# Signalling from TensorE by a drain behind each group of matmuls

## The reference

```python
x = layer_norm(dense_t @ Wd.T, gd, bd)                      # 2048 x 128
y = layer_norm(einsum('bnd,ed->bne', sparse_t, Ws), gs, bs)  # 26 rows of 64 -> 26 x 128
y = einsum('bne,pn->bep', y, Wsi)                           # 26 -> 32
y = swapaxes(layer_norm(y, gsi, bsi), 1, 2)
T = concatenate([x[:, None, :], y], axis=1)                 # 33 vectors of 128
Z = einsum('bnd,bmd->bnm', T, T)                            # their products
z = layer_norm(Z[:, TRIL_I, TRIL_J] @ Wl.T, gl, bl)[:, :384]
h = maximum(concatenate([z, dense_t]) @ W_top1 + b_top1, 0)
h = maximum(h @ W_top2 + b_top2, 0)
y = h @ W_top3                                              # 2048 x 1
```

## Time and profile before

| what | value |
|---|---|
| time, median of 3 runs | 772.6 us (771.04 to 772.69) |
| profiled execution, span | 1160.8 us |
| its own time beside the span | none is given |
| TensorE matmuls busy | 677.3 us (58%), 3847 |
| TensorE weight loads busy | 530.5 us (46%), 3847 |
| VectorE busy | 581.9 us (50%) |
| ScalarE busy | 480.7 us (41%) |
| GpSimd busy | 400.3 us (34%) |

### The profile page before, as it was taken

The page is one execution under the profiler, slowest core; times in us unless marked ns, Lnnn a source line. Parts: engine busy times, 40 slices in busy tenths (PEclk is TensorE's granted clock), DMA queues, the critical chain, the costliest instruction groups (busy, mean ns, idle before and its releaser), DMA issues.

```text
span 1160.8 us, 12848 instructions
## 1 busy us (share of the span) xinstructions
PE 677.3 (58%) x3847; PEld 530.5 (46%) x3847; DVE 581.9 (50%) x1124; ACT 480.7 (41%) x1459; POOL 400.3 (34%) x436
## 2 busy tenths in 40 slices
PE   5035446739184672927638374672927558388887
PEld 4023333727164371725517263461715437176664
DVE  4126536627274462727437165452717547188850
ACT  1004634525245252515436154342515526157753
POOL 6735252351705325070431706234070432500000
PEclk9558777969688797878859788795978869689998
DMA  8101010010100001010000101000010000100000
GB/s 312 25 16 18 12 19 11 10 20 3 26 3 17 13 10 21 0 26 3 15 14 3 26 0 21 8 12 17 1 26 2 16 14 8 22 1 1 1 1 1
DMA packets 15585, 22.55 MB, mean 19 GB/s; under 512 B 7461, under 2 KB 8127, under 8 KB 15039
## 3 DMA queue, kind: packets, MB, share of 16 engines
q0 software_dynamic: 13312, 13.66, 6.1%
q1 hardware_dynamic: 2240, 8.50, 2.0%
HBM read 22.12 MB, written 0.01 MB: 19 GB/s over the span
## 4 chain that ended last, share of the span: by engine, by line
PE 33%; another core or an unknown queue 28%; ACT 20%; issue 15%; DVE 4%; ACTq 0%; DVEq 0%
ACT zd L898 14%; PE bank_z L697 10%; PE bank_z L685 7%; ACT mixed L922 4%; PE bank_b L656 3%; PE bank_z L759 2%; PE bank_d L748 2%; PE bank_z L646 2%; PE bank_c L656 2%; PE bank_b L732 1%; PE bank_c L732 1%; DVE y L414 1%; PE bank_c L733 1%; DVE mixed L402 1%
## 5 line engine op out<-in xcount | busy, mean ns | idle before, releaser
L574 POOL DMA_INDIRECT rows<-in_table,ids x416 | 396.3, 953 | 135.0 <-issue 122.7
L898 ACT COPY zd<-bank_z 32x96 f32<-32x96 f32 (+3 forms) x768 | 194.1, 253 | 260.2 <-remote 151.8
L392 DVE COPY zd<-bank_z 32x96 f32<-32x96 f32 (+3 forms) x384 | 103.0, 268 | 212.6 <-remote 151.3
L646 PE MATMUL bank_z<-ident,rows 128*128 128x128 f32 x208 | 44.3, 343 | 278.7 <-ACT zd L898 165.3
L646 PEld LDWEIGHTS bank_z<-ident,rows 128*128 128x128 f32 x208 | 33.5, 181 | 300.5 <-issue 139.9
L568 POOL TENSOR_TENSOR ids<-ids_all,row_base 128x26 int32<-128x26 int32 x16 | 3.8, 236 | 473.9 <-DVE scaled L472 470.9
L697 PE MATMUL bank_z<-wl,zd 128*128 128x512 f32 x288 | 155.9, 675 | 6.6 <-ACT zd L898 6.6
L685 PE MATMUL bank_z<-r_vec 128*128 128x133 f32 x1024 | 135.4, 290 | 27.6 <-ACT zd L898 12.4
L685 PEld LDWEIGHTS bank_z<-r_vec 128*128 128x128 f32 x1024 | 131.2, 202 | 32.5 <-issue 17.0
L906 ACT ACTIVATE y_sq<-y 128x512 f32<-128x512 f32 x128 | 75.3, 625 | 90.0 <-DVE y L414 89.9
L732 PE MATMUL bank_b<-mixed,proj_hi 128*128 128x512 f32 x64 | 46.6, 729 | 100.7 <-DVE y L414 62.2
(11 more groups left out here) (114 smaller groups left out, 1004.0 us busy)
## 6 DMA issues: line engine op xcount, KB each, us to landing
rows<-in_table,ids POOLq DMA_INDIRECT x416
wl<-in_wl SPq DMA_DIRECT2D x1, 2304.0 KB
dense_t<-in_dense_t SPq DMA_DIRECT2D x1, 2048.0 KB
w<-in_w SPq DMA_DIRECT2D x1, 1280.0 KB
wsi_b<-in_wsi_b SPq DMA_DIRECT2D x1, 1248.0 KB
w<-in_w SPq DMA_DIRECT2D x1, 512.0 KB
mask_b<-in_mask_b SPq DMA_DIRECT2D x1, 288.0 KB
ids_all<-in_ids SPq DMA_DIRECT2D x1, 208.0 KB, 2.3
```

The costliest lines, as they stand in the source:

```text
L392: ins = v.tensor_copy(to, src)
L574: nc.gpsimd.indirect_dma_start(rows[par][:, c, D * blk:D * (blk + 1)], None, io["table"], bass.IndirectOffsetOnAxis(ap=ids[par][:, n:n + 1 ...
L646: mm = pe.transpose(bank_t[g % 2][:, n * P:(n + 1) * P], rows[par][:, c, :], ident[:])
L898: ins = nc.scalar.copy(to, src)
```

## The change

In ten helpers of TensorE's `tile_work` the increment is taken off the last matmul (or transposition) and put on a drain instruction that follows it. All are of the same form; these two stand for all ten (`turn`, `gram_product`, `interact`, `linear`, `turn_z`, `mix`, `project`, `first_layer`, `second_layer`, `third_layer`). In `project` there is one drain for each of the two halves; in `linear` and `first_layer` one behind the last piece alone. The waits, the order, the buffers and the matmuls of the set-up are as before.

```diff
                     for n, c in enumerate(GROUPS[g]):
-                        mm = pe.transpose(bank_t[g % 2][:, n * P:(n + 1) * P], rows[par][:, c, :], ident[:])
-                    mm.then_inc(turned, 1)
+                        pe.transpose(bank_t[g % 2][:, n * P:(n + 1) * P], rows[par][:, c, :], ident[:])
+                    pe.drain().then_inc(turned, 1)
...
                         pe.matmul(bank_g[blk][:], proj_hi[:], mixed[:, j % 2, blk, :], start=True, stop=False)
-                        pe.matmul(bank_g[blk][:], proj_lo[:], mixed[:, j % 2, blk, :], start=False, stop=True)\
-                            .then_inc(y_done, 1)
+                        pe.matmul(bank_g[blk][:], proj_lo[:], mixed[:, j % 2, blk, :], start=False, stop=True)
+                        pe.drain().then_inc(y_done, 1)
```

More of the change, by code:

```diff
@@ L655, in gram_product @@
                     for n, c in enumerate(GROUPS[g]):
-                        mm = pe.matmul(bank_g[g % 2][:, n * P:(n + 1) * P], rows_t[:, c, :], gram[:],
+                        pe.matmul(bank_g[g % 2][:, n * P:(n + 1) * P], rows_t[:, c, :], gram[:],
                                        start=True, stop=True)
-                    mm.then_inc(gram_done, 1)
+                    pe.drain().then_inc(gram_done, 1)
                 def z_banks_free(batches):
@@ L684, in interact @@
                     for n in range(per_bank * ZBANKS):
-                        mm = pe.matmul(bank_z[:, n // per_bank, (n % per_bank) * ZCOLS:(n % per_bank + 1) * ZCOLS],
+                        pe.matmul(bank_z[:, n // per_bank, (n % per_bank) * ZCOLS:(n % per_bank + 1) * ZCOLS],
                                        r_vec[:, first + n, OTHERS:ZCOLS], r_vec[:, first + n, :], start=True, stop=True)
-                    mm.then_inc(z_done, 1)
+                    pe.drain().then_inc(z_done, 1)
                 def linear(steps):
@@ L696, in linear @@
                     for s in steps:
-                        mm = pe.matmul(bank_l, zd[:, s, :], wl[:, s, :], start=(s == 0), stop=(s == STEPS - 1))
+                        pe.matmul(bank_l, zd[:, s, :], wl[:, s, :], start=(s == 0), stop=(s == STEPS - 1))
                     if steps[-1] == STEPS - 1:
-                        mm.then_inc(l_done, 1)
+                        pe.drain().then_inc(l_done, 1)
                 def turn_z():
@@ L703, in turn_z @@
                     for c in range(3):
-                        mm = pe.transpose(bank_l[:, c * P:(c + 1) * P], z_row[:, c * P:(c + 1) * P], ident[:])
-                    mm.then_inc(z_turned, 1)
+                        pe.transpose(bank_l[:, c * P:(c + 1) * P], z_row[:, c * P:(c + 1) * P], ident[:])
+                    pe.drain().then_inc(z_turned, 1)
                 def mix(j):
@@ L718, in mix @@
                         o = (s0 - j * SPB) * PROJ
-                        mm = pe.matmul(bank_m[j % 2][:, o:o + k * PROJ], scaled[:, c, :], wsi_b[:, w0:w0 + k, :],
+                        pe.matmul(bank_m[j % 2][:, o:o + k * PROJ], scaled[:, c, :], wsi_b[:, w0:w0 + k, :],
                                        start=(n == 0), stop=(n == len(wins) - 1), skip_group_check=True)
-                    mm.then_inc(mix_done, 1)
+                    pe.drain().then_inc(mix_done, 1)
                 def project(j):
@@ L747, in first_layer @@
                     for c in range(5):
-                        mm = pe.matmul(bank_d[:, k * TILE:(k + 1) * TILE], w1[:, c, k * P:(k + 1) * P],
+                        pe.matmul(bank_d[:, k * TILE:(k + 1) * TILE], w1[:, c, k * P:(k + 1) * P],
                                        z_t[:, c, :] if c < 3 else dense[c - 3], start=(c == 0), stop=(c == 4))
                     if k == 3:
-                        mm.then_inc(h1_done, 1)
+                        pe.drain().then_inc(h1_done, 1)
                 def second_layer():
@@ L758, in second_layer @@
                         for c in range(4):
-                            mm = pe.matmul(bank_w[:, k * TILE:(k + 1) * TILE], w2[:, c, k * P:(k + 1) * P], h1[:, c, :],
+                            pe.matmul(bank_w[:, k * TILE:(k + 1) * TILE], w2[:, c, k * P:(k + 1) * P], h1[:, c, :],
                                            start=(c == 0), stop=(c == 3))
-                    mm.then_inc(h2_done, 1)
+                    pe.drain().then_inc(h2_done, 1)
                 def third_layer():
@@ L765, in third_layer @@
                     for c in range(2):
-                        mm = pe.matmul(bank_w[0:1, 0:TILE], w3[:, c:c + 1], h2[:, c, :], start=(c == 0), stop=(c == 1))
-                    mm.then_inc(out_done, 1)
+                        pe.matmul(bank_w[0:1, 0:TILE], w3[:, c:c + 1], h2[:, c, :], start=(c == 0), stop=(c == 1))
+                    pe.drain().then_inc(out_done, 1)
                 if load:
```

## The result

The changed kernel takes 887.72 us (median of 3 runs, 887.7 to 890.82), the kernel before 772.6 us. The ratio is 1.1516 (95% interval 1.1489 to 1.1542): slower by 115 us, where 117 were forecast.

A forecast was written before the change was run, and what follows sets the result against it. TensorE was taken to bound two thirds of the round, ScalarE three places between. Drains 95, waits 12, signals 2.4, clock 13, ends -5 make 117 us on 772.6: 890 us, range 830 to 950.

The forecast's parts named there:

- The sum: Whole kernel: drains, waits, signals, clock and ends add 117 us to 772.6; the undisturbed round goes from 43.3 to 50.6 us.
- One drain: TensorE group boundary: matmul tail 0.22 us plus cold start 0.11, 0.33 us; 288 such drains make 95 us.
- The cheap drain: Rival at group boundaries: each drain costs the matmul's tail alone, 0.16 us; 46 us in all, 819 us; chance 0.12.
- 10 and 18: Per tile, 10 of 28 drains fall into TensorE's idle time and cost nothing; the other 18 pay in full.
- Waits and register work: TensorE's sequencer behind drains: second waits come into the open, 8 us, and threshold work in the loop, 4 us: 12 us.
- Later signals: Three interact hand-overs to ScalarE a tile are signalled 0.05 us later each: 2.4 us.
- The clock: TensorE's added idle time brings one more half-speed stretch of 1.8 us every second round: 13 us.
- The rival in which the clock collapses: Gaps in TensorE's closed stretch make half speed common, three more stretches a round: 76 us instead of 13, 953 us; chance 0.17.
- The ends: Last two rounds and set-up: TensorE waits more there, so drains go into idle time: -5 us.
- The base: Stalls during row gathering, 379 of 388 us, belong to the profiled execution only; so costs add to 772.6 us.
- Not slower: Rival at group boundaries: the next group's loads and matmuls pass the drain, only signals move: 772.6 us; chance 0.03.
- More cover: Rival: ScalarE or VectorE bounds parts of TensorE's stretch, hiding half the 288 drains: 63 us, 836 us; chance 0.12.

The follow-up runs named there:

- the bare drains: Kernel before plus a drain signalling nothing behind seven of second_layer's eight matmuls, 112 in all: 801.42 us, ratio 1.0396; on the chip with stalls 1214.9 us.
- the ten: Kernel before with only the 10 drains a tile that the prediction put into TensorE's idle time: 760.41 us against 771.31, ratio 0.986.
- the 18 alone: Kernel before with only the other 18 drains a tile, those predicted to lie outside TensorE's idle time: 897.29 us, ratio 1.1637.
- own signals: Changed kernel, but each last matmul keeps its increment and the drain behind it signals nothing: 889.33 us against 771.31 for the kernel before, ratio 1.1531.
- the kernel with waits behind the seven drains: As the bare drains, plus two satisfied waits behind each drain: 850.26 us, ratio 1.1033 to the kernel before; on the chip with stalls 1252.13 us.
- the kernel with the added waits alone: Kernel before plus the two satisfied waits in second_layer, without drains: 1180.47 us against 1182.78 on the chip with stalls, ratio 1.0005.

## Why the prediction was right, and where it wasn't

**The sum.** 117 us forecast, 115 measured. The round that answers to the earlier trace rows takes 50.5 us where 50.6 were forecast. The round shown with no fall is 49.3 against 42.0 us, 7.3 us more; the prediction's terms for a round, without the clock, were 18 x 0.33 + 12 / 16 + 0.15 = 6.8. With 0.34 us a drain and 0.09 a wait they are 18 x 0.34 + 10 x 0.09 + 0.15 = 7.2. That the sum came within 2 us is in part luck: the waits were put 6 us too low and the clock 7 us too high.

**One drain.** 0.33 us forecast, from the drain at the program's end and a cold start; 0.34 measured with the bare drains. The cheap drain (the tail alone) is refuted: with it the 112 bare drains would have made 18 us, and less still once the clock's 10 us are taken off, where 30.6 were measured. The Trainium skill, "Perfetto Trace Analysis", section "Sequencer-only Instruction (DRAIN, etc)", lets nothing be fetched before the drain is done; the trace with bare drains agrees, for TensorE's weight loads stand idle for 0.27 us behind each pair.

**10 and 18.** Right in what it says of the drains: the ten are free by the round's length (42.0 us both ways), and the 18 alone cost as much as all. What the cover gave up was 0.65, 0.88 and 1.08 us of the 1.97, 1.42 and 2.12, under the 1.0, 1.0 and 1.3 that I had, the first by a third.

**Waits and register work.** 0.051 us was too low for a group's second wait: behind a drain, the two waits added to the seven drains cost 0.09 together. This part of the term would be 14 us and not 8. The 4 us for register work in the loop weren't measured by themselves.

**Later signals.** 2.4 us forecast, and not to be told from nothing: with own signals the ratio is 1.1531, with the drains' 1.1516.

**The clock.** The term of + 13 us was too large, and wrong in its reason. A fall costs 1.5 us and not 1.8. I had one in every round of the kernel before, from the one round that I looked at; it is 8 in 14. And I had read the drains in the idle times only as more idle time; the ten drains there broke it into pieces, and by themselves they took the falls away. In the changed kernel that works against the gaps of the other 18, which alone bring the time at half speed from 72 to 109 us. Its clock over the span is 0.952, that of the kernel before 0.953: (1 - 0.952) / 0.5 x 885.9 = 85 against 72 us at half speed, four falls, 6 us in place of 13. That a fall costs 1.5 us in the changed kernel too is taken over from the kernel before. The rival in which the clock collapses didn't come, but the kernel with waits behind the seven drains shows that it could have: 22 falls, 32 us.

**The ends.** The - 5 us for the last rounds has the right sign. From the start of the 14th to that of the 16th instruction of L976 it is 78.3 us in the kernel before and 83.0 in the changed one, 4.7 us more for two rounds, where two middle rounds have 15.

**The base.** I took the stalls as something of the profiled execution. That step failed. The same kernel, unchanged, has a span of 769.2 us in one profile, and on another chip its timed runs take 1183 us. The sum held all the same, since the runs that the kernels were compared by had no stalls, and the stalls overlay the work without changing it. Whether the changed kernel stalls on such a chip wasn't tried, and what the stalls are stays open. Of the two comparisons there with drains added, the bare drains give the same increase in microseconds on either chip (32 and 30.6), those with waits a smaller one (69 and 79). All runs with stalls in their timed executions are of one chip and one session, so that it is the chip, and not something else about that session, isn't shown either.

**The rivals.** "Not slower" is refuted by the idle times of 0.23 us at group boundaries. "More cover": the 18 would have to cost half; they cost it all.

## What to carry to other kernels

Leave the increment on the matmul: a drain costs some 0.34 us of TensorE wherever work is queued behind it, and the waits and register work of the next group come into the open as well. Where TensorE is idle anyway a drain is free, and what decides then is what the idle time does to the clock. So before pricing a stall on TensorE ask two things: is there cover, and is the clock at full speed behind it.

## What the runs showed of the hardware

- Seven drains a tile inside idle time made the kernel faster by 1.4% (ratio 0.9862, 0.9841 to 0.9883), though all that the traces show of them is that waits of 2.1 to 2.4 us are broken into pieces. The clock then stayed at full speed from 130 to 700 us. A fall of 3.4 us costs 1.5 us, and the kernel before has 8 of them between 130 and 700 us. To mend only one of two such idle times (ratio 1.0037) left 8 falls, all behind the other. Waits as long stand in rounds without a fall, too (2.07 and 2.38 us).
- The same program ran in 771 to 772 us on three chips and in 1183 us on a fourth, run after run in one session (17 runs, 1165 to 1192). The extra time is in the rounds in which rows are gathered. In the profile of the kernel with the added waits alone, taken there, these last 67 to 73 us, and the two middle rounds without gathering 43.2 and 42.0, as elsewhere.
